# Weighing of the values of a 16-head biased cross-attention carried into the next head, with two accumulator banks and loops over pairs of heads

## What is computed

```
for each head h of 16:
    s[h]   = q[h] @ k[h].T * 16**-0.5 + fside[h]      # 128 x 12544, fside is a 1 x 16 x 128 x 12544 input
    p[h]   = exp(s[h] - rowmax(s[h]))
    att[h] = (p[h] @ v[h]) / rowsum(p[h])             # 128 x 16
x = x + concat(att) @ Wo + bo
```

## Time and profile before

| | us |
|---|---|
| median of 3 runs | 3363.52 |
| lowest and highest of them | 3355.19, 3363.97 |
| profiled execution, its own time | 3362.06 |
| its span in the profile | 3360.3 |
| second layer's head loop, first exp to last copy of the bank | 1079.3 to 1546.8 |

### The profile page before, as it was taken

One profiled execution on the slowest core, in us unless ns is written; L12 is line 12 of the kernel. 1 busy time (PEld: TensorE's weight loads), 2 busy tenths in 40 slices (PEclk: granted clock), 3 DMA queues, 4 the chain that ended last, 5 costly groups with the idle time before them and its releaser, 6 DMA issues. The chain is left out here.

```text
span 3360.3 us, 66618 instructions
## 1 busy us (share of the span) xinstructions
PE 3062.3 (91%) x23749; PEld 1948.1 (58%) x23749; DVE 1485.1 (44%) x4104; ACT 1453.5 (43%) x2501; POOL 246.9 (7%) x178
## 2 busy tenths in 40 slices
PE   8999999998787999995699999999999887999989
PEld 4555555556475666663445555555555675666678
DVE  2222222221424788885433333333333225888632
ACT  2323222223222888883144444444444432565621
POOL 2313232220000000000000000000000002000000
PEclk9999999999897999997899999999999987999979
DMA  6787878878238999970611111111111244665355
GB/s 212 255 257 255 252 257 248 257 243 277 86 120 312 357 353 356 356 309 21 241 40 39 57 57 38 57 57 38 57 57 38 83 165 120 154 155 146 98 180 197
DMA packets 298888, 576.42 MB, mean 172 GB/s; under 512 B 75522, under 2 KB 245288, under 8 KB 287528
## 3 DMA queue, kind: packets, MB, share of 16 engines
q1 hardware_dynamic: 298804, 575.31, 50.9%
HBM read 394.29 MB, written 180.97 MB: 171 GB/s over the span
## 5 line engine op out<-in xcount | busy, mean ns | idle before, releaser
L1558 DVE TENSOR_SCALAR_CACHE_REDUCE all_S<-l2x_scores 128x448 f32<-128x448 f32 x448 | 261.0, 619 | 413.7 <-PE l2x_scores L1473 413.7
L1460 PE MATMUL l2x_key_bank<-l2x_ctxT,l2x_wk_cur 128*64 128x448 f32 x1792 | 386.2, 552 | 3.0 <-DVE l2x_q_all L1602 1.4
L339 PE MATMUL prep_work<-prep_wv,prep_ctxT 128*128 128x512 f32 x784 | 341.5, 594 | 0.0
L1622 ACT COPY l2x_keys<-l2x_key_bank 128x448 f32<-128x448 f32 x224 | 119.2, 532 | 488.3 <-PE l2x_key_bank L1460 486.4
L705 DVE CUSTOM_DVE_ANT_0 all_S<-l1x_scores,l1x_bias 128x448 f32<-128x448 f32 x448 | 261.5, 620 | 56.1 <-PE l1x_scores L617 51.6
L960 DVE TENSOR_REDUCE l3x_rowmax<-l3x_scores 128x1 f32<-128x448 f32 x448 | 263.4, 622 | 39.7 <-PE l3x_scores L880 38.1
L1042 ACT ACTIVATE l3x_pT<-l3x_turned 128x896 f32<-128x896 f32 x224 | 205.0, 917 | 169.3 <-PE l3x_turned L888 166.0
L1496 PEld LDWEIGHTS l2x_out<-l2x_pT,l2x_v_half 128*64 128x64 f32 x3136 | 203.5, 137 | 96.7 <-issue 96.5
L774 ACT ACTIVATE all_S<-all_S,l1x_negmax 128x896 f32<-128x896 f32 x224 | 232.9, 1043 | 53.2 <-DVE l1x_negmax L718 33.5
L339 PEld LDWEIGHTS prep_work<-prep_wv,prep_ctxT 128*128 128x128 f32 x784 | 147.9, 190 | 185.4 <-issue 174.1
L1460 PEld LDWEIGHTS l2x_key_bank<-l2x_ctxT,l2x_wk_cur 128*64 128x64 f32 x1792 | 108.9, 136 | 245.2 <-issue 245.2
(11 more groups left out here) (647 smaller groups left out, 4241.3 us busy)
## 6 DMA issues: line engine op xcount, KB each, us to landing
l1x_bias<-in_fside_Bx16xSxS_dram SPq DMA_DIRECT2D x112, 896.0 KB, 6.8
scratch_k<-prep_kparts SPq DMA_DIRECT2D x84, 672.0 KB, 3.3
l1x_k_half<-scratch_k SPq DMA_DIRECT2D x32, 1568.0 KB, 9.6
l2x_v_half<-scratch_v SPq DMA_DIRECT2D x32, 1568.0 KB, 6.3
l3x_k<-scratch_k SPq DMA_DIRECT2D x32, 1176.0 KB, 7.3
scratch_v<-prep_st_v SPq DMA_DIRECT2D x14, 2048.0 KB, 9.3
scratch_k<-prep_kparts SPq DMA_DIRECT2D x56, 448.0 KB, 4.6
scratch_v<-prep_st_v SPq DMA_DIRECT2D x14, 1536.0 KB, 7.2
```

The costliest lines, as they stand in the source:

```text
L339: last = nc.tensor.matmul(w[:, h, :], ctxT[:, k, j * P:(j + 1) * P], wv2[:, k, h * 512:(h + 1) * 512], start=(k == 0), stop=(k == KT - 1))
L1460: last = nc.tensor.matmul(keys_ps[half * VW:(half + 1) * VW, 0:HB], wk_cur[:, k, :], ctxT[:, k, (2 * c + half) * HB:(2 * c + half + 1) * H ...
L1558: nc.vector.tensor_scalar(com.S[:, b * HB:(b + 1) * HB], scores_ps[half][:, 0:HB], 1.0, -3.4e38, ALU.mult, ALU.max, accum_out=rowmax[:, b: ...
```

## The change

`head_stream` is cut into two functions. The one for the first layer keeps its order. The one for the second layer, `head_stream_biased`, does this:

- The last five groups of head h are no longer weighed at the end of the head. They are weighed in the first five groups of head h+1, one in each, behind the scores. The sum over the four strips stands behind the weighing in group 6.
- There are two accumulator banks, `out` and `last`, used by turns, and the sum of the strips goes to columns 128 to 143 of the same bank.
- On VectorE the copy of the bank and the reciprocal stand behind group 5 of the next head (`leave_bank`), the division behind group 7 (`divide`). Behind the maximum only the total of the row sums is left (`sum_of`).
- The loops of TensorE and VectorE run over pairs of heads, since the bank must be a constant in the code.

```diff
-    def tensor_head(pe, h, following):
-        for c in range(GRP + lag):
-            if c < GRP:
-                turn(pe, h, c)
-                if following:
-                    scores(pe, h + 1, c)
+    def tensor_head(pe, h, odd, first=False, following=True):
+        for c in range(GRP):
+            turn(pe, h, c)
+            if following:
+                scores(pe, h + 1, c)
             if c >= lag:
-                weigh(pe, h, c - lag)
-        if tiles > 1:
-            sum_tiles(pe, h)
...
+                weigh(pe, h, odd, c - lag)
+            elif not first:
+                weigh(pe, h - 1, 1 - odd, c - lag + GRP)
+            if c == lag + 1 and not first:
+                sum_tiles(pe, h - 1, 1 - odd)
...
-        if heads > 1:
-            with pe.Fori(0, heads - 1) as h:
-                before_scores(pe, h + 1)
-                tensor_head(pe, h, True)
-        tensor_head(pe, heads - 1, False)
+        tensor_head(pe, 0, 0, first=True)
+        with pe.Fori(0, HEADS // 2 - 1) as i:
+            tensor_head(pe, i * 2 + 1, 1)
+            tensor_head(pe, i * 2 + 2, 0)
+        tensor_head(pe, HEADS - 1, 1, following=False)
+        for c in range(GRP - lag, GRP):
+            weigh(pe, HEADS - 1, 1, c)
+        sum_tiles(pe, HEADS - 1, 1)
...
-    def leave(dve, h):
+    def sum_of(dve, h):
 
         dve.wait_ge(exp_done, h * GRP + GRP)
         nc.vector.reduce_sum(total[:, :], rowsum[:, :], AX).then_inc(rowsum_taken, 1)
+
+    def leave_bank(dve, h, odd):
+        dve.wait_ge(weighed, h * GRP + GRP + ring)
+        nc.vector.tensor_copy(out_parts[:, :], banks[odd][:, 0:P]).then_inc(parts_ready, 1)
         dve.wait_ge(rowsum_taken, h + 2)
         nc.vector.reciprocal(inverse[:, :], total[:, :]).then_inc(out_step, 1)
+
+    def divide(dve, h, odd):
         dve.wait_ge(out_step, h + 1)
...
+        dve.wait_ge(summed, h + 1)
+        nc.vector.tensor_scalar(att[:, bass.ds(h * VW, VW)], banks[odd][:, P:P + VW], inverse[:, 0:1], None,
                                 ALU.mult).then_inc(out_taken, 1)
...
             if following:
                 take_scores(dve, h + 1, c)
+            if c == lag and not first:
+                leave_bank(dve, h - 1, 1 - odd)
+            if c == lag + 2 and not first:
+                divide(dve, h - 1, 1 - odd)
         if following:
             max_of(dve, h + 1)
-        leave(dve, h)
+        sum_of(dve, h)
```

More of the change, by code:

```diff
@@ L531, in head_stream @@
     copied = {"v": S("copied_by_vector"), "s": S("copied_by_scalar")}
[L532 to L535 removed]
+    v_loaded = [S(f"v_loaded{c}") for c in range(GRP)]
     by = ["v" if c in by_vector else "s" for c in range(GRP)]
[L537 removed]
     rank = [by[:c + 1].count(by[c]) for c in range(GRP)]
[L539 removed]
     class Run:
@@ L543, in head_stream, with on_sync @@
     run = Run()
[L544 to L550, removed]
+    run.out_taken = out_taken
+    def on_sync(sp):
+        for c in range(GRP):
+            j, at = c // (GRP // 2), c % (GRP // 2)
+            sp.dma_start(v_half[j][:, at * GC:(at + 1) * GC, :], v_src(c)).then_inc(v_loaded[c], 16)
@@ new lines, in on_scalar @@
+    def on_scalar(act):
+        act.wait_ge(negmax_ready, 1)
+        for c in range(GRP + 2):
+            if c < GRP:
+                s = com.S[:, c * GW:(c + 1) * GW]
+                nc.scalar.activation(s, s, ACT.Exp, bias=negmax[:, 0:1], scale=1.0,
+                                     accum_out=rowsum[:, c:c + 1]).then_inc(exp_done, 1)
+            if c >= 2 and by[c - 2] == "s":
+                copy_turned(act, nc.scalar.copy, c - 2)
+    run.on_sync, run.on_tensor, run.on_vector, run.on_scalar = on_sync, on_tensor, on_vector, on_scalar
@@ L575, in load_head, with load_values @@
[L575 to L590, removed]
+        def load_values(h, j, first):
+            if not first:
+                hold(sp, held, weighed, (h - 1) * GRP + GRP // 2 * (j + 1) + ring)
+            sp.dma_start(v_half[j][:, :, :], v_src(h, j)).then_inc(v_loaded[j], 16)
@@ new lines, in load_head @@
+        def load_head(k, v, first=False):
+            for i in range(GRP // 2):
+                if k is not None:
+                    load_bias(k, i, first)
+                    if i == 2:
+                        load_keys(k, 0, first)
+                    if i == 6:
+                        load_keys(k, 1, first)
+                if v is not None:
+                    if i == 3:
+                        load_values(v, 0, first)
+                    if i == 6:
+                        load_values(v, 1, first)
@@ L673, in on_tensor @@
-    def on_tensor(pe, before_scores=lambda pe, h: None):
-        if tiles > 1:
-            pe.wait_ge(cleared, 1)
-        if more_scores:
-            before_scores(pe, 0)
-            for c in range(GRP):
-                if ctx_loaded is not None and c % 2 == 0:
-                    pe.wait_ge(ctx_loaded[c // 2], 16)
-                scores(pe, 0, c)
-        if heads > 1:
-            with pe.Fori(0, heads - 1) as h:
-                before_scores(pe, h + 1)
-                tensor_head(pe, h, True)
-        tensor_head(pe, heads - 1, False)
+        nc.tensor.matmul(banks[odd][:, P:P + VW], out_parts[:, :], select[:, :], start=True, stop=True).then_inc(summed, 1)
```

262 lines of the change are left out of this document (141 added, 121 removed).

## The result

| | before | after |
|---|---|---|
| median of the runs made side by side, us | 3363.74 (4 runs) | 3410.06 (4 runs) |
| profiled execution, its own time | 3362.06 | 3411.02 |
| its span | 3360.3 | 3409.3 |

The changed kernel takes 1.014 times the time of the kernel before (95% interval 1.012 to 1.0161), 46 us more. The forecast was 3384 and its range ended at 3394: the sign was right, and the size was less than half of what came.

What follows compares the result with a forecast made beforehand. One closed chain of 29.27 us a head, paced by ScalarE first, later by TensorE at 1.84 us a group. 3362.06 + 10.9 (delay) + 10.5 (clock) = 3383.5, stated as 3384; range 3358 to 3394, the forecast's own 3374 to 3392.

Steps and rivals of the forecast that it cites:

- What bounds the stage, and the tail is worth 0: Head loop: one closed chain of 29.27 us; taking the tail off the boundary gains 0, group 0 starting at 1.26.
- faster: Rival, chance 0.12: TensorE carries the head's first half, so group 0's earlier start moves all that follows; about 3352 us.
- Groups 4 to 6: Five weighings moved into groups 0 to 4: group 4 at 8.85, 5 at 10.88, 6 at 12.72, 0.42 us late.
- VectorE in front of group 6: Bank copy and reciprocal ahead of VectorE's copy of group 6 add 0.36 us a head, between 0.19 and 0.45.
- The clock: TensorE idles 2.65 us at head boundaries; the clock halves at three of four, 1.0 us each: 10.5 us (0 to 19).
- Values and bias late: Loads of the values' second half and the bias tiles come later in the head; cost 0.
- Loops over pairs, fetch 0: TensorE's and VectorE's loops over two heads: instruction fetch at branches back put at 0, since no row showed one.
- The sum: Whole kernel: 3362.06 + 10.9 (delay) + 10.5 (clock) = 3383.5 us, stated as 3384.
- delay without the clock: Rival, chance 0.20: idle holes at the boundary do not lower the clock, only the 10.9 us delay comes; 3373 us.
- Fits in: Rival, chance 0.12: weighings and VectorE's part find room in the head and the clock holds; 3362 to 3364 us.
- Much slower: Rival, chance 0.08: transfers become the bound, or code is fetched at each branch back; 3395 us and above.

Runs made afterwards that it cites:

- the filler: 30 small matmuls leading to nothing on TensorE ahead of each head's first transposes, on the changed kernel with ScalarE's loop over two heads: 3367.67 us, ratio 1.002.
- the kernel with the halved loop: The changed kernel with ScalarE's second-layer loop over two heads instead of four: 3385.88 us, ratio 1.0059.
- the one with the loop moved back: The changed kernel with ten already satisfied waits ahead of ScalarE's loop over heads, so it begins at its old place: 3390.3 us, ratio 1.0072.

## Why the prediction was wrong

**What bounds the stage, and the tail is worth 0.** Right. Group 0 starts at 1.25 (1.26 forecast), and nothing of that reached the maximum. The rival "faster" falls by this. One reading was careless: in the earlier trace rows the exp comes 0.86 us behind its maximum (1167.98 - 1167.12), not 0.60. That head is an odd one; most heads of the kernel before show 0.58, so the 0.60, and what is worked out from it, stands.

**Groups 4 to 6.** Right: 8.84, 10.89 and 12.74 were measured for 8.85, 10.88 and 12.72.

**VectorE in front of group 6.** Mis-sized: 0.36 forecast, 0.1 measured. I had added two durations, 0.29 and 0.16. But VectorE starts an instruction before the one ahead of it has ended, and from the start of the bank's copy to the start of the next work there are 0.27 us (1153.18 to 1153.45). Part of these fell into idle time: the copy of group 6 starts 1.13 us behind its transposes (1153.70 - 1152.57), where it was 1.02. Together the delay is 29.79 - 29.27 = 0.52 a head, 14 x 0.52 = 7.3 us for 10.9, a little under the range's lower end of 8.5.

**The clock.** The mechanism is right and the filler shows it. The count was good too (ten of fourteen, 0.71 for 0.75), and so was the idle time, 2.14 to 2.42 us for 2.65. The price was too low: 1.33 us for the head read above and 1.5 on average, for 1.0. I subtracted 0.23 as absorbed in front of group 4, and that absorption does not last to group 5. It costs 14 x (30.87 - 29.79) = 15.1 us in the kernel with the halved loop, 14 x (31.00 - 29.79) = 16.9 in the one with the loop moved back (its interval of 32.88 among them); 10.5 were forecast.

**Values and bias late.** Cost 0, as forecast: no wait of TensorE or VectorE for a load is in the loop's waits after.

**Loops over pairs, fetch 0.** This is the step that failed, by a term of 21.6 us put at nothing, and in a way that the step did not ask about. I looked at TensorE's loop of the fourth layer, found no wait, and gave 0. I looked at no other engine and not at code placement. The stall fell on ScalarE, whose source in this stage the change does not touch, because five instructions went from its program a stage earlier. With it the loop costs 14 x (32.54 - 31.00) = 21.6 us more. The pair loops are free in the changed kernel by luck of place on VectorE, and cost 39 us in the kernel before. The Trainium skill ("Runtime: NRT & Kernel Launch", Instruction fetch mechanics) has the rule that a branch to code not held makes the engine wait for a fetch. I cited it and set it aside because no row showed it, which is weak evidence: none could show it as long as every loop of the stage was held. It names no price for the wait, so my "some us" stood on nothing; measured are 5 to 9 us a branch back. The page speaks of blocks of 256 instructions, two of them held, for such an engine. By these runs the pieces are 8 KB and a held part of three of them fits every start tried: with blocks of 256, 254 would have been as good a start as 194 and 224.

**The sum.** 7.3 + 16.9 + 21.6 = 45.8, measured 46.3. The three are differences from one kernel to the next, so they add up to the loop's 45.8 by themselves; what each stands for rests on the edit between the two kernels. Without the stalls it would be 24 us, or about 3388, inside the forecast's own range of 3374 to 3392; the kernels without stalls came out at 3390.3 and 3385.88. Of the rivals, "delay without the clock" falls by the windows at 0.50. "Fits in", which the busy share of the weight loads spoke for, falls by the same 0.44 us at group 6. "Much slower" had "a fetch at each branch back" as its last words, at 0.08 together with the transfers. It was the case that came, and it deserved a term and a price of its own.

## What to carry to other kernels

Count each engine's instructions ahead of each loop, before and after a change, also on engines and stages that it does not mean to touch. A loop that just fits what is held can cost 5 to 9 us at each branch back after a shift of its start, here of five instructions; at the one bad place where it was tried, half the body ended that. An idle stretch of 2.1 us on TensorE ahead of dense work can cost 1.5 us in clock each time, so leave work there and take it from where the engine sets the pace. Read that place from the starts of the groups, since a unit of work removed from a group that another engine paces frees nothing.

## What the runs showed of the hardware

- Code came to ScalarE and VectorE in packets of 8 KB (59 packets, 0.48 MB). A loop of 331 to 338 instructions ran free from starts 194, 224 (ScalarE), 452 and 488 (VectorE), and stalled at every branch back from 189, 254 (ScalarE) and 380 (VectorE). Starts and lengths are counted in the compiled program.
- A stall stood in the rows as 4.5 to 5.8 us on ScalarE (some 1.3 of them its ordinary wait), at start 189 with another 3.6 to 3.9 behind the next exp, and as about 7 us on VectorE. It shows as idle time released by "issue", and in no wait on a semaphore. Some four more packets on queue 14 come with each, but the third layer's loop had such packets without a stall.
- While ScalarE stalls twice, TensorE stands still for some 9 us (9.08 at 1209.18, for the ordinary 2.14), and then pays at the lower clock as well: after the stall at 1200.40 seven transposes took 1.75 us.
- TensorE's matmuls idle for 2.14 us at a boundary were followed by the lower clock (0.50, 1.2 GHz) in some heads (1170.90) and not in others (1141.00), with the same work around it. What decides it in one head I did not settle.
